# Making layer 2's folded values in the first stage instead of in layer 0's feed-forward stage

## What is computed

```python
x = x + tanh(g_xattn[0]) * _L0_xattn_ref(_layernorm(x), ctx_1024)        # first stage
x = x + tanh(g_ffn[0]) * _L0_ffn_ref(_layernorm(x), w_gate, w_up, w_down)  # second stage
...
# layer 2's attention, 16 heads of 64:
q = (xn @ w_q).reshape(B, SQ, NUM_HEADS, DIM_HEAD)
kv = context @ w_kv
k, v = split(kv, 2)
attn = softmax(einsum('bqhd,bkhd->bhqk', q * SCALE, k))
out = einsum('bhqk,bkhd->bqhd', attn, v).reshape(B, SQ, INNER) @ w_out + b_out
```

## Time and profile before

| what | value |
|---|---|
| time, median of 3 runs | 1223.0 us (1222.43 to 1223.14) |
| time of the profiled execution | 1222.84 us |
| span of its profile | 1221.0 us |
| first stage, 0 to 108.2 us: busy TensorE / VectorE / ScalarE | 74.30 / 75.38 / 56.63 us |
| second stage, 108.2 to 287 us: the same | 161.77 / 150.04 / 74.62 us |
| granted TensorE clock in the two stages, as a share of 2.4 GHz | 0.91 / 0.95 |

### The profile page before, as it was taken

One profiled execution on the slowest core, in us unless ns is written; L12 is line 12 of the kernel. 1 busy time (PEld: TensorE's weight loads), 2 busy tenths in 40 slices (PEclk: granted clock), 3 DMA queues, 4 the chain that ended last, 5 costly groups with the idle time before them and its releaser, 6 DMA issues. The chain is left out here.

```text
span 1221.0 us, 18803 instructions
## 1 busy us (share of the span) xinstructions
PE 1076.0 (88%) x6180; PEld 904.8 (74%) x6180; DVE 801.5 (66%) x1816; ACT 521.1 (43%) x1190; POOL 163.9 (13%) x224
## 2 busy tenths in 40 slices
PE   4786799997999879988999977999778989989996
PEld 3664477776888758877888846888657878878886
DVE  5687889876777554457887676776545554655543
ACT  3565444433444454434655513555333423323221
POOL 2221000001111050230000021122115000000000
PEclk9887899999999989989999998999879999999998
DMA  9201010001000000000000050000011211211222
GB/s 292 63 1 37 1 11 1 1 1 69 1 0 0 1 11 1 0 1 1 2 0 0 1 220 1 1 0 1 1 62 49 66 44 53 61 47 50 61 69 70
DMA packets 30278, 41.18 MB, mean 34 GB/s; under 512 B 13520, under 2 KB 19482, under 8 KB 29319
## 3 DMA queue, kind: packets, MB, share of 16 engines
q1 hardware_dynamic: 29341, 39.63, 10.4%
q10 hardware_dynamic: 873, 0.72, 0.2%
HBM read 37.80 MB, written 2.54 MB: 33 GB/s over the span
## 5 line engine op out<-in xcount | busy, mean ns | idle before, releaser
L347 ACT COPY work<-psum 128x256 f32<-128x256 f32 (+2 forms) x256 | 105.0, 433 | 209.1 <-PE psum L336 203.0
L298 POOL TENSOR_TENSOR rstd<-ve,mhalf 128x1 f32<-128x1 f32 x128 | 80.8, 631 | 800.2 <-DVE ve L293 800.2
L336 PE MATMUL psum<-ident,work 128*128 128x128 f32 (+1 forms) x656 | 115.3, 289 | 43.0 <-DVE work L303 10.3
L336 PEld LDWEIGHTS psum<-ident,work 128*128 128x128 f32 (+1 forms) x656 | 79.1, 148 | 73.1 <-issue 14.2
L2040 DVE TENSOR_TENSOR work<-psum,work 128x512 f32<-128x512 f32 x68 | 47.0, 691 | 101.6 <-ACT work L1977 101.5
L1470 PE MATMUL psum<-early,work 128*128 128x352 f32 x256 | 84.9, 489 | 6.7 <-ACT zone L478 4.0
L1910 PE MATMUL psum<-x_hi,ew_hi 128*128 128x512 f32 (+1 forms) x272 | 88.0, 405 | 2.6 <-ACT work L1977 2.6
L1980 ACT CAST h_hi<-work 128x512 fp32r<-128x512 f32 x68 | 42.2, 620 | 110.7 <-DVE work L2045 100.3
L1910 PE MATMUL psum<-x_lo,ew_hi 128*128 128x512 f32 (+1 forms) x272 | 85.5, 396 | 0.0
L1910 PE MATMUL psum<-x_hi,ew_lo 128*128 128x512 f32 (+1 forms) x272 | 84.9, 394 | 0.0
L1920 PE MATMUL psum<-ew_hi,h_hi 128*128 128x256 f32 x272 | 76.6, 281 | 4.2 <-DVE x L2057 3.8
(11 more groups left out here) (253 smaller groups left out, 2537.8 us busy)
## 6 DMA issues: line engine op xcount, KB each, us to landing
work<-expert_shares SPq DMA_DIRECT2D x64, 256.0 KB, 3.2
early<-in_experts_in SPq DMA_DIRECT2D x1, 6528.0 KB, 18.5
x<-in_x_in SPq DMA_DIRECT2D x4, 512.0 KB, 6.7
early<-in_W_in SPq DMA_DIRECT2D x2, 1024.0 KB, 5.9
out_x<-x SPq DMA_DIRECT2D x1, 2048.0 KB, 7.5
early<-in_Wk SPq DMA_DIRECT2D x1, 1024.0 KB, 6.1
early<-in_Wq SPq DMA_DIRECT2D x1, 1024.0 KB, 8.8
zone<-in_Wv SPq DMA_DIRECT2D x1, 1024.0 KB, 14.0
```

Source lines behind the costliest of these rows:

```text
L298: pool.tensor_tensor(rstd[:, slot:slot + 1], ve[:, slot:slot + 1], mhalf[:, 0:1], ALU.pow).then_inc(s["rstd_ready"], 1)
L336: last = pe.transpose(dst[0:rows, at:at + n], src, ident[0:n, 0:n])
L347: act.copy(dst, src).then_inc(s["tr_copied"], 1)
```

## The change

The 20 tiles of VO are made by the first stage, as set-up units in its steps 11 to 16, and no longer by the second. To have the values ready for it, the set-up units of steps 5 to 16 stand in another order: layer 2's keys are done by step 6, the turned query weights by step 9, the values in steps 9 and 10, and the folded keys in steps 12 to 16 beside the folded values. The area `v_even` moves to the second half of VO itself, and one of the two parts of `v_odd` to where layer 2's key weights stood. Two of the three areas are set to zero by GpSimd before the first stage's steps, the third in its step 11. In the second stage TensorE's and ScalarE's steps 4 to 11 become a hardware loop of four turns over pairs of steps.

```diff
-        v_even = early[:, FP4_END:FP4_END + B * VP].rearrange("p (b x) -> p b x", b=B)
-        v_odd = (early[:, FP4_END + B * VP:FP4_END + (B + 1) * VP],
+        v_even = VO[:, KT:, :].rearrange("p a b -> p (a b)").rearrange("p (b x) -> p b x", b=B)
+        v_odd = (early[:, FP4_END + 8 * D:FP4_END + 8 * D + VP],
                  zone13[:, 2 * B * HK + B * KT * 3 * VW[3] + 4 * D:][:, 0:VP])
...
-        FOLDS = {10: 2, 11: 3, 12: 4, 13: 4, 14: 3}
-        VALUES = {14: 1, 15: 4, 16: 3}
+        KEYS = {5: 3, 6: 5}
+        TURNS = {8: 4, 9: 4}
+        VALUES = {9: 2, 10: 6}
+        OUTS = {11: 4, 12: 3, 13: 3, 14: 3, 15: 3, 16: 4}
+        FOLDS = {12: 3, 13: 3, 14: 3, 15: 4, 16: 3}
...
+                if t == 11:
+                    pe.wait_ge(ld["wo"], 16 * 3)
+                    pe.wait_ge(set_s["read"], KEYS_UNITS + 1 + 8 + 2 + 8)
+                for _ in range(OUTS.get(t, 0)):
+                    unit(fold_values, count["outs"] // KT, count["outs"] % KT)
+                    count["outs"] += 1
                 if t in (5, 8, 11):
...
+                if t == 11:
+                    pool.wait_ge(set_s["filled"], KEYS_UNITS)
+                    pool.memset(v_odd[0], 0.0).then_inc(set_s["vp_zero"], 1)
-            pool.wait_ge(set_s["filled"], TURNED_UNITS)
-            pool.memset(v_even, 0.0).then_inc(set_s["vp_zero"], 1)
-            for v in v_odd:
-                pool.memset(v, 0.0).then_inc(set_s["vp_zero"], 1)
...
-                for i in range(vo_units(t)):
-                    wait(pe, s["tr_copied"], tr.n - 1)
-                    fold_values(pe, bank[TR45[tr.odd]], *vo_unit(t, i)).then_inc(s["tr_filled"], 1)
-                    tr.up()
-
-            pipeline(pe, -2, step, (), T + 1)
+
+            pipeline(pe, -2, step, [(tr, 6)], T + 1, 3)
```

More of the change, by code:

```diff
@@ L532, in take_wide_values @@
             return last
[L534 to L542, removed]
         def fold_values(pe, dst, bb, k):
@@ L843, in unit @@
                 un.up()
-            folds = wide = 0
+            count = dict.fromkeys(("keys", "turns", "values", "folds", "outs"), 0)
             def setup_units(t):
-                nonlocal folds, wide
                 if t == 2:
@@ L858, in setup_units @@
                     pe.wait_ge(ld["wk2"], 16)
-                if t in (5, 6, 7):
-                    for j in range(3 * t - 15, min(8, 3 * t - 12)):
-                        unit(project_keys, 2, j)
+                for _ in range(KEYS.get(t, 0)):
+                    unit(project_keys, 2, count["keys"])
+                    count["keys"] += 1
                 if t == 7:
@@ L937, in setup_units @@
                     key_split_scalar(act, 1)
-                if t in (5, 6, 7):
-                    for j in range(3 * t - 15, min(8, 3 * t - 12)):
-                        unit(take_wide_keys, j)
+                for _ in range(KEYS.get(t, 0)):
+                    unit(take_wide_keys, count["keys"])
+                    count["keys"] += 1
                 if t == 7:
@@ L1533, in step @@
                     key_split_scalar(act, 3)
[L1534 to L1539, removed]
+            pipeline(act, -4, step, [(tr, 6)], T + 1, 3)
             end_stage(act, "act")
@@ L1587, in step @@
                     tr.up()
-                for _ in range(vo_units(t)):
-                    tr.up()
                 if has(t + 5):
@@ L1594, in step @@
                                              ALU.mult, ALU.mult).then_inc(s["nmr_ready"], 1)
-            pipeline(dve, -5, step, [(tr, 6 + 2 * VO_UNITS), (chain_n, 2 * (4 + 2 + 2))], T + 2, 5)
+            pipeline(dve, -5, step, [(tr, 6), (chain_n, 2 * (4 + 2 + 2))], T + 2, 5)
             end_stage(dve, "dve")
```

56 lines of the change are left out of this document (30 added, 26 removed).

## The result

The changed kernel takes 1230.42 us (median of 9 runs, 1226.92 to 1231.88), the kernel before 1222.43 in the same runs (9, 1221.93 to 1225.32): ratio 1.0056, 95% interval 1.0043 to 1.007. It is 8 us slower, where 1223.1 with 1220.2 to 1226.6 was forecast. The profiled execution took 1230.83 us (span 1229.0).

A forecast was written before the change was run, and what follows sets the result against it. No one engine was taken to fill the first stage, and TensorE to pace the second. A first-stage loss of 9.7 us and second-stage gain of 9.6 made +0.1 us: 1223.1 us, range 1220.2 to 1226.6.

The forecast's parts named there:

- That only two stages change: Whole kernel: stages meet at a barrier, so the two stage differences, +9.7 and -9.6 us, simply add to +0.1.
- First stage, +9.7: First stage: following TensorE through steps 9 to 16, its end moves from 108.1 to 117.8 us.
- step 9 was to begin at 70.2: First stage: step 9's units start at 70.2 us instead of 71.71, following an earlier query column and scaling.
- the 2.1 credited: First stage: the query column starts about 54.0 instead of 56.09, so the scaling behind it ends 2.1 us earlier.
- everything before that is untouched by the change: First stage: up to step 7, where GpSimd's late root holds VectorE 8.68 us to 48.42, the change alters nothing.
- 47.6 were summed with handovers: First stage, steps 9 to 16: TensorE's work summed from 70.2 to 117.8 us, including 1.2 for handovers with ScalarE.
- adding products plus 1.36: First stage: a step's length is its products plus 1.36 us of own work; the prediction fails if steps 11-16 don't.
- It is less than the 14.6 that comes in because three things lie free: First stage: loss is 9.7 us through a shortened 4.15 us VectorE operation, filled TensorE waits and vanished slow last value units.
- Second stage, gain 9.6: Second stage: without 14.6 us of products VectorE sets the pace, gaining 9.6 us (bounds 7.0 to 10.5).
- The zeroing at nothing: First stage: GpSimd's two early zero writes stay hidden, the third beside VectorE's subtraction costs 0, at most 1.2 us.
- A second fall in steps 9 to 16 of the first stage: Slower rival: TensorE's clock drops again in step 9, costing about 2 us; total 1225.1 to 1225.6; 12%.
- the other three: Rivals: TensorE doesn't catch up in second stage, 1226.4 (13%); first stage takes units for less, 1220.1 (17%); nothing moves.

The follow-up runs named there:

- fill: Changed kernel plus 16 unread TensorE products of 128x256 in the pauses at the start of layer 1's attention; 1228.22 us against 1231.05 without them.
- delay1: Changed kernel plus five chained 64-column copies on ScalarE at the end of the first stage, a pure delay; 1230.12 us.
- before_c: Kernel before, unaltered, in its third execution with a trace; the three repeats took 1223.98, 1223.91 and 1222.88 us.
- no_outs: Changed kernel with the 20 units of folded values made nowhere (ScalarE copies a constant tile instead); 1213.78 us, ratio 0.9913.
- split12: Changed kernel with 12 folded-value units returned to layer 0's FFN and 8 left in the first stage; 1220.07 us, ratio to before 0.9975.
- split: Changed kernel with ten folded-value units returned to layer 0's FFN and ten left in the first stage; 1219.95 us, ratio to before 0.9979.
- no_products: Kernel before without TensorE's products for layer 2's folded values in the second stage (ScalarE copies a constant tile); 1215.39 us, ratio 0.9946.
- after_c: Changed kernel, unaltered, in its third execution with a trace; this and the fourth took 1228.72 and 1230.71 us.

## Why the prediction was wrong

The forecast was +0.1 us. By the means of four traces each the whole is 7.0 us longer (8.0 by the medians of nine runs each): the first stage takes 3.8 us more than summed, the unchanged stages 3.3, and the second stage is right within 0.2. So two steps failed, about equally; in the pair of traces above it is 3.3 and 5.0.

*That only two stages change, "and I add the two differences".* Stage lengths don't just add: the change moved all later work by 2.9 us, TensorE's clock met two unchanged pauses at another moment, and 3.6 and 2.1 us were lost in unchanged code (2.8 and 1.2 more than before's own mean). No rival covered it; mine had the clock fall inside the first stage only. That the loss is there and is the clock's is shown by fill and the eight traces; that the moment decides rests on delay1 and on where the falls meet the work.

*First stage, +9.7.* Mis-sized: 13.0 in the pair, 13.5 on the mean. Part one: step 9 was to begin at 70.2 and began at 72.2 to 72.8. I had it hang on the query column. The column started late, at 55.67 and not 54.0, but the scaling behind it ended at 60.61 + 2.19 = 62.80, 2.7 us earlier than before and not the 2.1 credited. What held step 9 was another chain. ScalarE's row behind the scaling:

```profile
60.61 2.19 ACT L942 ACTIVATE early<-early,zone 128x1024 f32<-128x1024 f32 x2
...
66.00 0.94 ACT L689 ACTIVATE work<-work,minus_magic 128x768 f32<-128x768 f32 x1 [2.56 <-DVE work L677]
```

This rounding stands ahead of the copies of the turned query tiles and waits for VectorE, and VectorE was late from the root on that GpSimd delivers late. I wrote that everything before that is untouched by the change; its order is, its time isn't. GpSimd stands behind a DMA transfer, before and after:

```profile
47.34 0.46 POOL L621 TENSOR_TENSOR zone<-zone,pmask 128x160 f32<-128x160 f32 x1 [14.51 <-DMA zone<-v_pairs]
```

```profile
49.07 0.47 POOL L611 TENSOR_TENSOR zone<-zone,pmask 128x160 f32<-128x160 f32 x1 [16.42 <-DMA zone<-v_pairs]
```

Of the 2.0 us at step 9, 1.7 are there already. In all 18 traces VectorE's next norm (48.42 before, 50.16 after) starts 1.1 us behind the row of GpSimd and has the rounding's input ready 15.8 us later. The transfer carries what TensorE makes at 35 us, and it makes it at full clock in before's trace and at half in after's:

```profile
35.00 1.03 PE L507 MATMUL psum<-zone,ctxT 128*77 128x256 f32 x4
```

```profile
35.32 1.91 PE L507 MATMUL psum<-zone,ctxT 128*77 128x256 f32 x4
```

The clock first rose at 32.9 us in before's trace and at 40.9 in after's. The split is the same in all 18 traces: in the eight with a rise between 32.0 and 34.9 that norm starts at 48.2 to 49.6, in the ten with a rise between 38.1 and 41.9 at 50.2 to 51.3. All four traces of the changed kernel had the late rise, but delay1, the same kernel up to its copies, had the early one: its step 9 begins at 71.43 and its first stage is done at 120.24. Before is not hurt by the late rise, since its scaling, which then meets a faster query column, ends earlier (63.57 in before_c, 65.46 in its first trace). Whether the change makes a late rise likelier is open.

Part two: the steps 9 to 16 took 121.07 - 72.23 = 48.8 us (in each trace of this arrangement), where 47.6 were summed with handovers. Steps 9 and 10 took 5.2 and 6.7 us for 4.5 and 5.8, as TensorE waits there for ScalarE six times; steps 11 to 16 took 34.4 for 33.3 without handovers. So adding products plus 1.36 is a sound account of steps where TensorE is full.

*"It is less than the 14.6 that comes in because three things lie free."* Mostly wrong. From step 9 to the end no_outs takes 34.4 us, with eight units 39.0 (split12), with ten 40.8, with twenty 48.8. So twenty units cost 14.4 us, nearly all of TensorE's 14.6; eight cost 4.7 (0.58 each, a little of it in TensorE's gaps), and beyond ten each costs 0.80, its full 0.73 with a handover. no_outs ends at 107.7 and not at 117.8 - 14.6 = 103.2: 3.1 of that is its late step 9 (73.3), the rest VectorE's other work in the last tiles. L653's operation did get short (L643: 0.19 us), without the stage following. (split's step 9 begins 1.2 us later than split12's, 72.20 against 70.97: 0.45 by the root, the rest with a clock that stayed low to 73.2 and not 69.5.)

*Second stage, gain 9.6.* Right: 10.1 in the pair of traces, 9.8 on the mean of four each, 9.7 in no_products. Steps 5 to 10 took 243.26 - 185.15 = 58.1 (58.2 summed), 11 and 12 18.8 (18.8), 13 to 15 22.8 (23.0); the waits for the rounding were 0.77 (0.8 assumed) and 0.56. TensorE turns tile 15 0.5 us behind VectorE, so it does catch up. From tile 5 on it is 9.4; the rest lies at the stage's start, which moves with the clock in before's traces too.

*The zeroing at nothing.* Right. At the start GpSimd's three writes take 3.89 us and its first root comes at 6.51 (6.80 to 6.88 in the other three traces), earlier than the 6.93 of before. The third stood beside VectorE's subtraction, with no effect on it:

```profile
57.80 1.16 POOL L1045 MEMSET early<- 128x1280 f32 x1
```

```profile
57.95 2.71 DVE L589 TENSOR_TENSOR kb_lo<-early,kb_hi 128x2464 fp32r<-128x2464 f32 x1
```

(one view each, GpSimd and VectorE; the operation took 2.71 us in before too, with no write beside it). The Trainium skill (SBUF — State Buffer, SBUF: two separate sides) has only a GpSimd operation that reads block a two-input operation of VectorE; the trace agrees. The long L653 of before is of another kind, with one input: it ended at 76.78 + 4.15 = 80.93, 0.05 us behind the last of GpSimd's three writes, and with no write beside it takes 0.19.

*The rivals.* A second fall in steps 9 to 16 of the first stage did not come: in after's trace the clock is 1.00 from 71.7 us to the stage's end. Nor did the other three.

What stays open: at which moments a pause brings the fall. The traces show a pair of falls for arrivals 2.7 to 3.4 us and 5.8 us behind before's, and a single one at 4.0, and that the changed kernel meets the bad moment in each of its four traces; a rule to foresee that, they don't give. Its untraced runs spread from 1226.92 to 1231.88 us, so it may not meet it in every execution. The differences past 460 us (after_c and no_products win 2.4 back near 900 in one trace each) were not followed.

## What to carry to other kernels

Work moved from a stage that TensorE bounds frees only the difference to the next engine (here 9.4 of 14.6 us), and in a stage with few gaps it costs most of its length from the first unit and all of it beyond the tenth (0.58, then 0.80 us for a unit of 0.73); so split it where both stages still have room (here 8 and 12), rather than move all. When work at a stage's end is moved forward, look at what each in-order engine waits for ahead of it: here a rounding on ScalarE that hangs on VectorE, a root, and a transfer. When the balance of a change is a few us, each later pause of TensorE may add or take 1 to 4 us through its clock, so the range has to be wider than the sum of the changed terms, and two kernels are compared by several traces of each. A filling longer than its pause costs time itself (3.9 us at the full clock, 5.6 as measured, in a pause of 2.71); a filling that fits was not tried.

## What was not expected of the hardware

A pause of 1.36 us was followed by 3.4 us of clock 0.50 in the changed kernel (293.5 to 296.9) and by none in before's first trace. A delay of 1.35 us put into the program did not make it measurably slower (1230.12 us against 1231.05, with ranges that overlap). And in the first stage the clock first rose at 32.9 to 41.0 us from one execution to the next, over the same work, which moved VectorE's norm behind the late root between 48.2 and 50.6 us in before, while the stage's end in its four traces moved by 0.7 us.
